# Column sums of a transposed context: GpSimd folds four blocks, TensorE multiplies once

## The reference

```python
# attention, per tile: hidden = layernorm(x), memory = ctx_2048
scores = einsum('bsd,bmd->bsm', hidden, memory) / sqrt(512)   # masked over m
x = x + einsum('bsm,bmd->bsd', softmax(scores), memory)
# network
h = silu(bitlinear158(layernorm(x), w1, b1))     # 512 -> 2048
h = gelu(h)                                      # exact gelu
h = layer_norm(h, ln_g, ln_b)
x = x + bitlinear158(h, w2, b2)                  # 2048 -> 512
# bitlinear158: rms_norm, rows rounded to 8 bits by their largest value,
# weights rounded to -1, 0, 1 by their mean absolute value
```

## Time and profile before

| what | value |
|---|---|
| median of 3 runs | 441.71 us (439.6 to 442.36) |
| profiled execution | 438.11 us, of which the span of the profile is 436.0 us |
| PE busy | 385.1 us (88%) |
| ACT busy | 383.9 us (88%) |
| DVE busy | 378.6 us (87%) |
| POOL busy | 274.9 us (63%) |
| granted TensorE clock, mean | 0.984 |

### The profile page before, as it was taken

The page is one execution under the profiler, slowest core; times in us unless marked ns, Lnnn a source line. Parts: engine busy times, 40 slices in busy tenths (PEclk is TensorE's granted clock), DMA queues, the critical chain, the costliest instruction groups (busy, mean ns, idle before and its releaser), DMA issues. The chain is left out here.

```text
span 436.0 us, 6941 instructions
## 1 busy us (share of the span) xinstructions
PE 385.1 (88%) x1878; PEld 204.0 (47%) x1878; DVE 378.6 (87%) x618; ACT 383.9 (88%) x519; POOL 274.9 (63%) x389
## 2 busy tenths in 40 slices
PE   3888899498999999989999899889979988889786
PEld 2655455244545554545455445545435543344332
DVE  6678478999899999989998898999978989999882
ACT  1549999999999999999999898999979999999930
POOL 4366757767395879564875568456566377657940
PEclk9999989989999999999999999999989999989999
DMA  8999991626648937658559586745937531262695
GB/s 302 401 324 326 337 288 43 152 96 136 180 95 219 207 114 177 182 131 231 117 177 206 117 198 142 224 87 161 230 84 181 86 84 25 50 134 48 137 201 147
DMA packets 110390, 73.88 MB, mean 169 GB/s; under 512 B 87048, under 2 KB 87056, under 8 KB 109584
## 3 DMA queue, kind: packets, MB, share of 16 engines
q1 hardware_dynamic: 110352, 73.43, 63.9%
HBM read 44.05 MB, written 8.39 MB: 120 GB/s over the span
## 5 line engine op out<-in xcount | busy, mean ns | idle before, releaser
L608 PE MATMUL z<-w1q,q1T 128*128 128x512 f16 x512 | 123.0, 384 | 5.5 <-DMA q1T<-q 2.7
L633 PE MATMUL acc<-w2q,q2T 128*128 128x512 f16 x512 | 119.0, 383 | 4.4 <-DMA q2T<-hid 4.3
L608 PEld LDWEIGHTS z<-w1q,q1T 128*128 128x128 f16 x512 | 49.1, 99 | 67.3 <-issue 11.0
L633 PEld LDWEIGHTS acc<-w2q,q2T 128*128 128x128 f16 x512 | 49.8, 99 | 64.1 <-DMA q2T<-hid 6.7
L1893 DVE SCALAR_TENSOR_TENSOR hid<-hid,nmu,gain 128x2048 f32<-128x2048 f32 x32 | 78.5, 2454 | 0.5 <-issue 0.5
L1902 DVE SCALAR_TENSOR_TENSOR hid<-hid,rstd,beta 128x2048 f32<-128x2048 f32 x32 | 75.6, 2363 | 2.3 <-POOL rstd L1513 2.1
L1124 ACT ACTIVATE hid<-z,fac 128x1024 f32<-128x1024 f32 x64 | 70.6, 1112 | 2.6 <-PE z L613 2.2
L1907 DVE TENSOR_REDUCE am<-hid 128x1 f32<-128x2048 f32 x32 | 72.5, 2270 | 0.1
L1146 ACT ACTIVATE junk_l<-hid 128x2048 bf16<-128x2048 f32 x32 | 60.9, 1904 | 7.6 <-DVE hid L1902 7.6
L1526 POOL TENSOR_SCALAR hid<-hid,kq 128x2048 f16<-128x2048 f32 x30 | 62.7, 2091 | 2.1 <-DVE kq L1916 1.9
L1135 ACT ACTIVATE junk_v<-hid,gsum 128x2048 bf16<-128x2048 f32 x32 | 63.7, 1990 | 0.1
(11 more groups left out here) (102 smaller groups left out, 570.2 us busy)
## 6 DMA issues: line engine op xcount, KB each, us to landing
ctxT<-in_ctxT_dram SPq DMA_DIRECT2D x32, 256.0 KB, 3.2
xs<-in_x_dram SPq DMA_DIRECT2D x32, 256.0 KB, 3.5
ctx<-in_ctx_dram SPq DMA_DIRECT2D x32, 256.0 KB, 3.5
xT<-in_xT_dram SPq DMA_DIRECT2D x32, 256.0 KB, 3.3
out_dram<-xs SPq DMA_DIRECT2D x32, 256.0 KB, 2.4
hid<-in_w1T_dram SPq DMA_DIRECT2D x4, 1024.0 KB, 8.8
hid<-in_w2T_dram SPq DMA_DIRECT2D x4, 1024.0 KB, 9.5
gain<-in_g_dram SPq DMA_DIRECT2D x1, 1024.0 KB, 7.9
```

The lines of the kernel that those rows point to most:

```text
L608: pe.matmul(z_ps[h][:, c * CH:(c + 1) * CH], q1T[:, t % 4, k, :], w1q[:, k, f0:f0 + CH], start=(k == 0), stop=False)
L633: mm = pe.matmul(a, q2T[:, t % 2, c, :], w2q[:, c, :], start=False, stop=(c == FC - 1))
```

## The change

A new function on POOL, `fold_ctx(t)`, adds the four blocks of `ctxT` for a pair of tiles: first blocks 0 and 1 to blocks 2 and 3 (128x512 out), then the two halves of that (128x256 out). `column_sums(t)` is then one f32 product of 256 columns instead of four. The four buffers of `ctxT` are released by the fold (`s_fold`) instead of by the column sums. Two small buffers are new. The number of calls of every other function on every engine is the same.

```diff
+        chalf = sb("chalf", [P, 2, 2, P]); cfold = sb("cfold", [P, 2, 2, P])
...
             def load_ctxT(t):
                 wait(sp, s_score, t - 3)
-                wait(sp, s_csp, t // 2 - 1)
+                wait(sp, s_fold, t // 2 - 1)
...
                 wait(pe, s_corr, t)
-                pe.wait_ge(s_ctxT[t % 4], landed(t, 4))
-                pe.wait_ge(s_ctxT[t % 4 + 1], landed(t, 4))
-                for c in range(DC):
-                    mm = pe.matmul(csum_ps, neg[:, :], ctxT[:, t % 4:t % 4 + 2, c, :], start=(c == 0), stop=(c == DC - 1))
-                mm.then_inc(s_csp, 1)
+                pe.wait_ge(s_fold, t // 2 + 1)
+                pe.matmul(csum_ps, neg[:, :], cfold[:, t // 2 % 2, :, :], start=True, stop=True).then_inc(s_csp, 1)
...
+            def fold_ctx(t):
+
+                pool.wait_ge(s_ctxT[t % 4], landed(t, 4))
+                pool.wait_ge(s_ctxT[t % 4 + 1], landed(t, 4))
+                wait(pool, s_csp, t // 2 - 1)
+                s = ctxT[:, t % 4:t % 4 + 2, :, :]
+                pool.tensor_tensor(chalf[:, :, :, :], s[:, :, 0:2, :], s[:, :, 2:4, :], ALU.add).then_inc(s_half, 1)
+                pool.wait_ge(s_half, t // 2 + 1)
+                pool.tensor_tensor(cfold[:, t // 2 % 2, :, :], chalf[:, :, 0, :], chalf[:, :, 1, :], ALU.add).then_inc(s_fold, 1)
```

All five orders are written anew. In PE's and ACT's lists most calls between tiles 8 and 25 move by no more than three places; in POOL's they come later by the folds put between them. The beginning differs more. SP's list begins, before and after:

```diff
-            load_mask(0)
             load_ctxT(0)
-            load_mask(1)
-            load_w1(0)
-            load_b1()
             load_ctxT(1)
             load_x(0)
-            load_ctx(0)
-            load_x(1)
-            load_xT(0)
-            load_x(2)
-            load_w1(1)
-            load_xT(1)
             load_b2()
             load_ctxT(2)
+            load_xT(0)
+            load_x(1)
+            load_mask(0)
             load_ctxT(3)
+            load_w1(0)
+            load_xT(1)
+            load_x(2)
```

```diff
+            fold_ctx(0)
+            mask_bias(0)
             x_rstd(0, 2)
-            mask_bias(0)
+            x_rstd(2, 2)
+            fold_ctx(2)
             centre_x1(0)
-            x_rstd(2, 2)
             x1_rho(0, 1)
+            round_w1(0)
+            fold_ctx(4)
```

More of the change, by code:

```diff
@@ L759, in _ @@
             scores(10)
+            pe.wait_ge(s_silu[1], 6)
+            warm(10)
+            pe.wait_ge(s_centred, 11)
+            scores(11)
             pe.wait_ge(s_brow, 6)
@@ new lines, in _ @@
+            pe.wait_ge(s_corr, 20)
+            scores(18)
+            pe.wait_ge(s_turn, 18)
+            readout(17)
+            pe.wait_ge(s_centred, 19)
+            scores(19)
+            turn_factors(14)
+            second_product(8, 0)
+            pe.wait_ge(s_x1, 18)
+            turn_probs(18)
+            turn_factors(15)
+            second_product(8, 1)
+            second_product(9, 0)
+            pe.wait_ge(s_turn, 19)
+            turn_probs(19)
+            second_product(9, 1)
@@ new lines, in _ @@
+            pe.wait_ge(s_silu[0], 14)
+            first_product(14, 0)
+            pe.wait_ge(s_centred, 20)
+            column_sums(20)
+            pe.wait_ge(s_turn, 20)
+            readout(18)
+            pe.wait_ge(s_silu[1], 14)
+            first_product(14, 1)
+            pe.wait_ge(s_silu[0], 15)
+            first_product(15, 0)
+            pe.wait_ge(s_silu[1], 15)
+            first_product(15, 1)
+            turn_factors(16)
+            pe.wait_ge(s_corr, 22)
+            scores(20)
@@ new lines, in _ @@
+            turn_factors(17)
+            pe.wait_ge(s_x1, 19)
+            readout(19)
+            second_product(10, 0)
+            second_product(10, 1)
+            second_product(11, 0)
+            second_product(11, 1)
+            pe.wait_ge(s_centred, 21)
+            scores(21)
+            pe.wait_ge(s_x1, 20)
+            turn_probs(20)
+            pe.wait_ge(s_silu[0], 16)
+            first_product(16, 0)
+            pe.wait_ge(s_turn, 21)
+            readout(20)
+            pe.wait_ge(s_silu[1], 16)
@@ new lines, in _ @@
+            first_product(16, 1)
+            pe.wait_ge(s_centred, 22)
+            column_sums(22)
+            pe.wait_ge(s_silu[0], 17)
+            first_product(17, 0)
+            pe.wait_ge(s_x1, 21)
+            turn_probs(21)
+            pe.wait_ge(s_silu[1], 17)
+            first_product(17, 1)
+            pe.wait_ge(s_corr, 24)
+            scores(22)
+            pe.wait_ge(s_turn, 22)
+            readout(21)
+            pe.wait_ge(s_centred, 23)
+            scores(23)
+            turn_factors(18)
@@ new lines, in _ @@
+            readout(22)
+            first_product(18, 1)
+            pe.wait_ge(s_silu[0], 19)
+            first_product(19, 0)
+            pe.wait_ge(s_silu[1], 19)
+            first_product(19, 1)
+            turn_factors(20)
+            pe.wait_ge(s_corr, 26)
+            scores(24)
+            turn_factors(21)
+            pe.wait_ge(s_x1, 23)
+            readout(23)
+            second_product(14, 0)
+            second_product(14, 1)
+            second_product(15, 0)
+            pe.wait_ge(s_centred, 25)
@@ L1619, in _ @@
             round_q1(13)
+            centre_x1(14)
+            fold_ctx(18)
+            norm_kappa(8, 2)
+            centre_x1(15)
             gelu_mean(10)
-            centre_x1(14)
-            centre_x1(15)
-            norm_kappa(8, 2)
+            mask_bias(5)
             round_q2(8)
+            gelu_rstd(10, 2)
+            round_q1(14)
+            x1_rho(14, 2)
             gelu_mean(11)
-            gelu_rstd(10, 2)
-            x1_rho(14, 2)
             centre_x1(16)
@@ L2018, in _ @@
-            softmax(8)
+            x_stats(7)
+            add_readout(4)
+            add_readout(5)
+            clamp_w2(0)
+            softmax(6)
+            x1_absmax(4)
+            x_stats(8)
+            copy_factors(2)
+            clamp_w2(1)
+            x1_absmax(5)
+            softmax(7)
+            gained(0)
+            x_stats(9)
+            q1_scale(4, 2)
+            prob_sum(6)
+            add_readout(6)
+            z_scale(4, 2)
+            prob_sum(7)
+            invert_factors(4, 2)
```

1153 lines of the change are left out of this document (561 added, 592 removed).

## The result

| | kernel before | changed kernel |
|---|---|---|
| median | 440.65 us (438.3 to 442.36, 4 runs) | 452.31 us (451.46 to 452.83, 4 runs) |
| ratio, 95% interval | | 1.0249 [1.0199, 1.0299] |
| profiled execution, span | 438.11, 436.0 | 452.83, 450.8 |

What follows compares the result with a forecast made beforehand. ACT, 96% busy, was taken to bound the middle, between a load-set start and a waiting tail. Start -2.5, PE's relief -4.0, folds +1.0, DVE +0.5 gave -5.0 us: profiled 438.1 to 433.1, median 436.7, range 429.5 to 444.5.

Steps and rivals of the forecast that it cites:

- the price of a fold by POOL's idle time: Folds on POOL: idle time takes up most; 1.0 us reaches ACT for all sixteen, end points 0 and +11.
- the port wait inside a gap: POOL's wait for SBUF ports shared with DVE: 0.5 us per operation at a random moment, 1 us a fold.
- The upper end given, +11: Upper end of the folds' cost on ACT, in us, if four folds stand in the way.
- Fold cost on POOL: Each fold costs POOL some 3.0 us, 1.8 for additions with their hop and 1 for ports; sixteen cost 47 us.
- PE's relief: Middle, 80 to 400 us: fewer column sums on PE save 4.0 us of ACT's 5.5 us of waits owed by PE.
- The start: Before the first product: scores of tile 0 start 4 us earlier, near 9.5 us; 2.5 us are gained.
- DVE held up: Term: folds delay DVE through shared ports, +0.5 us. Rival of that name: folds hold DVE, no gain, about 444 us, chance 0.08.
- GpSimd late, slower: Rival: folds on POOL stand ahead of steps that DVE waits for, delaying ACT; 450 us, chance 0.12.
- ACT was the bound all along: Rival: PE's relief becomes PE's idle time and the start keeps its time; 440.7 us, chance 0.26.
- The lists find more: Rival: new orders remove all but two of ACT's 12.6 us idle, start gives 4 us; about 429 us, chance 0.14.

Runs made afterwards that it cites:

- experiment 3: Changed kernel's new orders without folds, one column-sum product per pair from the first block alone (sums incomplete): 440.32 us, 0.9947 of the kernel before.
- experiment 4: Kernel before in its own orders, folds put where POOL had stood idle, one product per pair, one ctxT load issued earlier: 451.49 us, ratio 1.0228.
- Experiments 10 and 11: Changed kernel with folds for the first eight tiles only, 445.06 us, 1.0091; and from tile 8 on only, 448.65 us, 1.0158; other pairs have four products.
- experiment 1: Changed kernel's new orders with the folds taken out and four products per pair as before: 444.97 us, 1.0029 of the kernel before.
- experiment 2: Kernel before in its old orders, column sums from the first of four blocks alone (sums incomplete), no folds: 442.62 us, ratio 1.0029.
- Experiment 8: Changed kernel with column_sums(2) behind readout(0) on PE, and fold_ctx(2) and centre_x1(0) ahead of x_rstd(2, 2) on POOL: 450.57 us, ratio 1.0198.
- experiment 6: Changed kernel with each fold replaced by two memsets of like length that read nothing, PE's product from the first block (sums incomplete): 446.81 us, ratio 1.0116.
- experiment 5: Changed kernel with the additions cut to 8 and 4 elements a partition, product from block 0 still behind the fold (sums incomplete): 438.02 us, ratio 0.9921.

## Why the prediction was wrong

**The failed step** is the price of a fold by POOL's idle time: "that idle time takes up most folds", "Where a fold falls into POOL's idle time it costs nothing", and 1.0 us on ACT for all sixteen. The runs show 13 us (experiment 3 against the changed kernel). The error is one of kind: 112 us of idle time in the middle were taken as a store from which any step may draw, while an engine with a fixed order has only the play at the place where the step stands, until the next step somebody waits for. At 157 us that play was 0.83 us for a fold of 2.07. The second half of the error is the port wait inside a gap. It was priced for a moment at random, 1.0 us a fold; the changed kernel shows 0.9, but over those twelve gaps of experiment 4 it is 1.8 in the mean and up to 4, as in the gap shown there, where DVE runs `gained` and `normed` while POOL would wait for ACT. Folds of 3.9 us in the mean met gaps of 3.1, so even the gaps themselves did not take up the folds. The upper end given, +11, was near what came; it was weighted as "four in the way", when 13 us over sixteen folds are 0.8 us for each, if all count alike. Experiments 10 and 11 agree with that: four folds cost 0.6 points and twelve 1.3.

**Fold cost on POOL: right.** 1.8 us unhindered and 1 us for ports were predicted, 47 us in all; 1.27 + 0.73 = 2.0 and 46.3 with the ports were measured. The sum went wrong not in the cost but in who pays. POOL as a whole came to 333.8 us, 14 above the forecast, and that is not the folds' doing: in experiment 3, the new orders without a fold, it is busy for 289.0 us against 274.9 before.

**PE's relief: right in size in the new orders only.** -4.0 predicted; some 3.6 us in experiment 3 against 1, within their intervals, and nothing in experiment 2. The reading of ACT's named waits gives what could be had at most, not what one gets without new orders. PE's group of column sums fell by 22.3 us (32.8 to 10.5) for 24.6 worked out, and PE's total was 369.7 us for 361.

**The start: wrong.** The first scores came at 9.79 us for 9.5 predicted, the constants and the fold as worked out. But the first silu is 4.5 us later, not 2.5 earlier. In the new orders it comes at 41.6 (experiment 3) and 43.0 us (experiment 1) without folds, 41.7 with folds of a few elements, 44.7 with folds, 44.9 with memsets and 51.9 with folds twice. That looks as if it followed what stands on POOL, but experiment 2 has it at 43.3 with POOL's list untouched, so 3 us of difference prove nothing here; only the 51.9 is clear of that. The start was priced for the loads and for PE; POOL's list, with three folds ahead of the first `round_q1`, was not walked through. At 17.11 POOL starts the second fold, and PE's list has the column sums that wait for it ahead of the first readout:

```profile
17.11 1.27 POOL L1511 TENSOR_TENSOR chalf<-ctxT 128x512 f32<-128x512 f32 x1
```

Experiment 8 changed that order and the first silu stayed where it was, so this wait alone is not the cause. The first product starts 4.8 us late and takes 1.3 us longer, at the lower clock; which step of the start holds it back stays open. What it costs in the end is small beside the rest: experiment 1, whose first silu is 2.8 us late, ends at 1.003.

**DVE held up: low.** +0.5 predicted. `gained` and `normed` together take 157.2 us, against 154.1 before, 154.0 in experiment 3 and 152.0 with folds of a few elements: 3 to 5 us, and experiment 6 against the changed kernel puts some 6 us on the reading of the additions in all. The prediction said that of POOL holding up DVE the old trace shows only tenths. That was a misreading: the earlier trace rows has a `gained` of 3.39 us, 1.05 above the median; it began at 300.78 us, when `round_q2` had been running on POOL since 300.06 (1.97 us). Beside the additions it shows more plainly, in the line view of `normed`, of the one long addition and then of the folds of a few elements:

```profile
L1980 DVE SCALAR_TENSOR_TENSOR hid<-hid,rstd,beta x32: 2328/2350/3941, 72.7 to 431.6; 128x2048 f32<-128x2048 f32 x32
```

```profile
L1982 DVE SCALAR_TENSOR_TENSOR hid<-hid,rstd,beta x32: 2329/2350/2787, 67.9 to 418.3; 128x2048 f32<-128x2048 f32 x32
```

One `normed` took 1.59 us longer than the median, most of the addition's 1.94: the addition had begun at 81.78 us, `normed` at 81.92. By the Trainium skill, SBUF — State Buffer, section "SBUF: two separate sides", whoever starts first holds the shared pair for the whole instruction, and a VectorE operation with two SBUF inputs meets it only in a GpSimd operation that reads SBUF. The rows agree with both halves: up to 3.94 us beside an addition, and 2.39 in the mean beside memsets, as without any fold (2.40 in experiment 3). `gained` reached 3.69 us beside memsets too, and in experiment 2 without any fold; it meets other steps of POOL that read, as at 300.78 us.

**The rivals.** "GpSimd late, slower" named the mechanism and nearly the time (450), at 0.12. It was held down by its "against", POOL's idle time of 112 us, which is no evidence. "DVE held up" is a smaller part of the same loss. "ACT was the bound all along" and "The lists find more" are out as forecasts of the time: ACT was busy for 9 us less in the middle. But of PE's relief in the old orders the first said what experiment 2 shows, that it becomes PE's idle time. The clock explains a small part at most. Among the 25 runs of the kernel before that stand beside experiments 1 to 4, a granted clock lower by 0.01 goes with some 2 us (a line through them; it doesn't say which causes which), and the changed kernel's four had 0.971 in the mean for 0.983. That would be 2 or 3 of the 11 us. The rest isn't the clock: experiment 4's profiled execution took 450.79 us at 0.981.

## What to carry to other kernels

Before work is put on an engine "with room", walk its list place by place: how long does the engine wait between this place and the next step that somebody needs, and is that wait longer than the new step with its wait for ports? The sum of its idle time says nothing; here 35% idle gave 1.2 us of play a pair, and beyond it each microsecond cost 0.9. Nor is a gap as wide as it looks when the new step shares ports with another engine: at nine of twelve gaps the folds of experiment 4 were stretched from 2.1 to about 4 us or more. If a step is just too long, halve it before giving it up: the first addition alone was nearly free, and the second, half as long, cost three times as much. But take the gain first as a run without its cost (one product, sums left out): it was 2 to 4 us against the kernel before (experiments 3 and 5), less than the folds' price.

## What the runs showed of the hardware

- An addition of two f32 tensors on POOL took 0.20 us for 4 or 8 columns, 0.73 for 256, 1.27 for 512 and 1.94 for 824: 0.2 us and 2.1 ns a column, where a one-input operation of 512 took 0.69. A memset to bf16 of 1408 columns took as long as the addition of 512.
- An addition of 4 or 8 columns, 0.20 us by itself, took 0.66 us in the mean of the 32 here, up to 2.33; memsets of 1.27 us at the same places never took more than 1.28, and those of 0.74 us took 1.23 at most.
- It goes both ways: in the kernel before, a one-input operation of 2048 columns on POOL that began 0.72 us earlier made a `gained` last 3.39 us for 2.34.
